# Expert bias of a routed feed-forward layer: split on GpSimd, both parts stacked in one 36-row operand

## The chip, the cores and the metric

One NeuronCore of one Trainium2 chip. The metric is device time in microseconds (us) of one execution. Times inside a trace are us from the start of the span, unless they are given in ns.

## The reference

For x of 2 x 128 tokens of width 512 and a context of 2 x 2048 tokens: x += cross-attention(layernorm(x), context), 16 heads; x += layernorm(self-attention(layernorm(x)) + its input); and a feed-forward layer in which each token goes to one of four experts. What the change touches is in that last part:

```
expert_idx = argmax(x @ W_router)                      # 4 experts
h = gelu(einsum('th,ehi->tei', x, W1) + b1)            # W1 [4, 512, 2048], b1 [4, 2048]
intermediate = einsum('te,tei->ti', onehot, h)
y = layernorm(intermediate @ Wo + bo + x)              # Wo [2048, 512]
```

## The kernel before

The kernel is one block in which each engine has a hand-written list of instructions, in order, tied by semaphores. All DMAs are issued by SyncE (SP), in the order of its own list.

Cross-attention runs to about 354 us. The self-attention that follows has its queries, keys and values in `qkvn` (VectorE adds the bias rows to the PSUM products at L609). They go to HBM and back in another layout (`qkvp`, L257 and L259). Then VectorE runs four additions with all operands in SBUF (`u` at L614, `x_sb` at L615, for each of two batches), one small memset, and the copies of the transposed keys from PSUM into the block-diagonal tile `KM` (L626), on which the score matmuls (L949) wait. `KM` was zeroed by GpSimd (L313) as soon as cross-attention's last weighted values were done. GpSimd otherwise does only the `rsqrt` of each layernorm (L293) there.

The feed-forward layer computes fp32 products from fp32r parts. An operand is split in two: the high part is a rounding copy, the low part is the difference. For tile n of sixteen (four experts, four k tiles each), `split_w1(n)` on VectorE writes `w1H` (L662) and `w1L` (L664) from `w1raw`, which has two buffers; PE then runs 24 matmuls of 512 columns (L1014 to L1016) into all eight PSUM banks: two batches, four column chunks, three part products. `zH` and `zL` are the tokens masked for one expert (`masked_tokens(e)`, L709), for expert 0 ahead of the tiles and for expert e + 1 after `split_w1(4e + 1)`. `split_w1(0)` is far ahead, at 438 us. VectorE may overwrite the buffers of tile n once PE has counted `w1_tile` for tile n - 2.

The bias enters as matmuls that open the accumulation of each bank: `ohT`, the transposed one-hot of the tokens (4 rows), against `b1H` and against `b1L` (4 x 2048 each), L1003. VectorE makes `b1H` (L699) and `b1L` (L701) between `yTL` (L696) and the evacuation of `ohT` (L703).

SP's list, in the order that matters: the last `rows` of biases after cross-attention (L253), the round trips of `qkvn` (L257, L259), `b1raw` (L260), the round trips of the attention's output, then W1 tile n as soon as `w1_split` counts n - 1, and after tile 3 the whole second matrix `woF` (4 MB, 32 KB in each partition, L273):

```python
sp.wait_ge(w1_split, n - 1)
sp.dma_start(w1raw[n % 2][:], w1_v[n]).then_inc(w1_in[n % 2], 16)
if n == 3:
    sp.wait_ge(o2_mm, B)
    sp.wait_ge(b1_split, 2)
    sp.dma_start(woF[:], a["ffn_Wo"]).then_inc(woF_in, 16)
```

The byte ranges matter too: `woF` takes 0 to 32 KB of each partition, `b1raw` 8 to 16 KB before the change.

Of the kernel before, what the change touches and what calls it, by code (L numbers as in the profile page):

```python
# [11 lines left out]
F32 = mybir.dt.float32  # L12
F32R = mybir.dt.float32r
ALU = mybir.AluOpType
# [9 lines left out]
def perceiver_block(nc, a, out):  # L24
# [23 lines left out]
    with ExitStack() as ctx:  # L48
# [3 lines left out]
        def at(name, shape, dtype, kb):  # L52
            return nc.alloc_sbuf_tensor_at(name, shape, dtype, offset=base + int(kb * KB))

        def sem(name):
            return ctx.enter_context(nc.semaphore(name))
# [57 lines left out]
        QT2 = at("QT2", [P, G2, P], F32, 185)  # L114
        zH = at("zH", [P, NW1, TOK], F32R, 136)
        zL = at("zL", [P, NW1, TOK], F32R, 152)
        b1raw = at("b1raw", [E, I], F32, 8)
        b1H = at("b1H", [E, I], F32R, 168)
        b1L = at("b1L", [E, I], F32R, 176)
        mask = at("mask", [P, E, TOK], F32, 185)  # L120
        ohT = at("ohT", [E, B, P], F32R, 189.5)
        wr = at("wr", [P, KT, E], F32, 191)
        hid = at("hid", [P, B, I], F32, 168)

# [5 lines left out]
        def cols(n):  # L130

            col[0] += n
            assert col[0] <= 384
            return small[:, col[0] - n:col[0]]
# [16 lines left out]
        order = cols(E)  # L151
        rank = cols(B * E).rearrange("p (b e) -> p b e", b=B)
        rmax = cols(B)
        onehot = cols(B * E).rearrange("p (b e) -> p b e", b=B)

        ps = ctx.enter_context(nc.psum_tensor("ps", [P, 8, CH], F32))
        T_BANKS = (4, 5)
# [2 lines left out]
        QK2_BANKS = (2, 0)  # L160
        CT_BANKS = (2, 0)
        NP = B * G
        HALF = KT // 2
        WARM = 14
        NOT_YET = 3.0e38
# [29 lines left out]
        cT_mm, cT_done, o2_mm, x2T_mm, x2T_done = (sem(n) for n in ("cT_mm", "cT_done", "o2_mm", "x2T_mm", "x2T_done"))  # L195
        logit_mm, z_ready, ohT_mm, ohT_ready, zT_mm = (sem(n) for n in ("logit_mm", "z_ready", "ohT_mm", "ohT_ready", "zT_mm"))
        z_hi, z_split, w1_hi, w1_split, b1_hi = (sem(n) for n in ("z_hi", "z_split", "w1_hi", "w1_split", "b1_hi"))
        b1_split, w1_tile, w1_mm, gelu_done, hT_mm = (sem(n) for n in ("b1_split", "w1_tile", "w1_mm", "gelu_done", "hT_mm"))
        hT_act, hT_dve, f_mm, out_ready, stored = (sem(n) for n in ("hT_act", "hT_dve", "f_mm", "out_ready", "stored"))
        yT_hi, yT_lo, mask_mm, mask_done, resid_done = (  # L200
            sem(n) for n in ("yT_hi", "yT_lo", "mask_mm", "mask_done", "resid_done"))
# [14 lines left out]
        @block.sync  # L216
        def _(sp):
            sp.dma_start(wk_raw[:, :, 0:P], a["xWk"][:, :, 0:P]).then_inc(wk_in, 16)
            for h in range(2):
                k = slice(HALF * h, HALF * (h + 1))  # L220
                sp.dma_start(raw[0][:, k, :], a["ctxT"][0][:, k, :]).then_inc(raw0_in[h], 16)
            sp.dma_start(bias3, a["bias3"]).then_inc(bias_in, 16)
            for h in range(2):
                k = slice(HALF * h, HALF * (h + 1))
                sp.dma_start(wv_raw[:, k, :], a["xWv"][:, k, :]).then_inc(wv_half_in[h], 16)
            sp.dma_start(x[:], a["x"].rearrange("b t d -> t b d")).then_inc(x_in, 16)
            sp.dma_start(raw[1][:], a["ctxT"][1]).then_inc(raw_in[1], 16)
            sp.dma_start(wq[:], a["xWq"]).then_inc(wq_in, 16)
            for c in range(2, C):
                sp.dma_start(raw[c][:], a["ctxT"][c]).then_inc(raw_in[c], 16)  # L230
            sp.dma_start(wk_raw[:, :, P:D], a["xWk"][:, :, P:D]).then_inc(wk_rest_in, 16)
            for c in range(C):

                sp.wait_ge(k_mm, C * (G - 1) + c + 1)
                sp.dma_start(raw[c][:], a["ctxT"][C + c]).then_inc(raw_in[c], 16)

            sp.wait_ge(v_mm, B * C * JT)
            sp.dma_start(wo[:], a["xWo"]).then_inc(wo_in, 16)
            sp.dma_start(wq2[:], a["wq"]).then_inc(wqkv2_in, 16)
            sp.wait_ge(k_mm, NP * C)  # L240
            sp.dma_start(wk2[:], a["wk"]).then_inc(wqkv2_in, 16)
            sp.dma_start(wv2[:], a["wv"]).then_inc(wqkv2_in, 16)
            sp.dma_start(wo2[:], a["wo"]).then_inc(wo2_in, 16)
            w1_v = a["W1"].rearrange("e (k p) i -> (e k) p i", p=P)
            for n in range(2):
                sp.dma_start(w1raw[n][:], w1_v[n]).then_inc(w1_in[n], 16)
            sp.wait_ge(s_mm, NP * C * HPG)
            for n in range(2):
                sp.dma_start(rowsA[:, n, :], a["rows"][n:n + 1, :].to_broadcast([P, D])).then_inc(rowsA_in, 16)
            sp.dma_start(wr[:], a["W_router"]).then_inc(wr_in, 16)  # L250
            sp.wait_ge(pv_mm, NP * C)
            for n in range(8):
                sp.dma_start(rows[:, n, :], a["rows"][2 + n:3 + n, :].to_broadcast([P, D])).then_inc(rows_in, 16)  # L253

            for b in range(B):
                sp.wait_ge(qkv_ready, 3 * (b + 1))
                sp.dma_start(qkv_by_token[b], qkvn[:, b, :, :]).then_inc(qkv_out[b], 16)  # L257
                sp.wait_ge(qkv_out[b], 16)
                sp.dma_start(qkvp[:, b, :, :, :], qkv_by_position[b]).then_inc(qkv_in[b], 16)  # L259
            sp.dma_start(b1raw[:], a["b1"]).then_inc(b1_in, 16)  # L260
            for b in range(B):
                sp.wait_ge(c2_ready, b + 1)
                sp.dma_start(c_by_position[b], c2[b][:]).then_inc(c2_out[b], 16)
                sp.wait_ge(c2_out[b], 16)
                sp.dma_start(cn[:, b, :], c_dram[b]).then_inc(c2_in[b], 16)
            for n in range(2, NW1):
                sp.wait_ge(w1_split, n - 1)
                sp.dma_start(w1raw[n % 2][:], w1_v[n]).then_inc(w1_in[n % 2], 16)
                if n == 3:

                    sp.wait_ge(o2_mm, B)
                    sp.wait_ge(b1_split, 2)
                    sp.dma_start(woF[:], a["ffn_Wo"]).then_inc(woF_in, 16)  # L273
            for b in range(B):
                sp.wait_ge(out_ready, b + 1)
                sp.dma_start(out[b], u[:, b, :]).then_inc(stored, 16)
            sp.wait_ge(stored, 16 * B)
# [3 lines left out]
        def _(pool):  # L281
            pool.memset(ident[:], 0.0).then_inc(ident_done, 1)
            pool.memset(minus_half, -0.5).then_inc(half_done, 1)
            for e in range(E):
                pool.memset(order[:, e:e + 1], float(E - e)).then_inc(half_done, 1)
            pool.wait_ge(ident_done, 1)
# [1 line left out]
                               pattern=[[-1, P]], channel_multiplier=1).then_inc(ident_done, 1)  # L288

            def rsqrt(n):  # L290
                pool.wait_ge(half_done, 1 + E)
                pool.wait_ge(var_done, n + 1)
                pool.tensor_tensor(rstd[:, n:n + 1], vareps[:, n:n + 1], minus_half, ALU.pow).then_inc(rstd_done, 1)  # L293

# [17 lines left out]
            pool.wait_ge(pv_mm, NP * C)  # L312
            pool.memset(KM[:], 0.0).then_inc(km_zero, 1)  # L313
            pool.wait_ge(km_zero, 1)
            for n in range(B, NLN):
                rsqrt(n)


# [130 lines left out]
        def _(dve):  # L449
# [206 lines left out]

            def split_w1(n):

                dve.wait_ge(w1_in[n % 2], 16 * (n // 2 + 1))
                if n >= 2:  # L660
                    dve.wait_ge(w1_tile, n - 1)
                dve.tensor_copy(w1H[n % 2][:], w1raw[n % 2][:]).then_inc(w1_hi, 1)  # L662
                dve.wait_ge(w1_hi, n + 1)
                dve.tensor_tensor(w1L[n % 2][:], w1raw[n % 2][:], w1H[n % 2][:].bitcast(F32),  # L664
                                  ALU.subtract).then_inc(w1_split, 1)
# [12 lines left out]
                statistics(x2[:, b, :], EPS, 2 * B + 2 * b + 1)  # L678
                normalize(x2[:, b, :], y[:, b, :], 2 * B + 2 * b + 1)

            dve.wait_ge(half_done, 1 + E)
            for b in range(B):
                dve.wait_ge(logit_mm, b + 1)
                step(dve.tensor_copy(logit[:, b, :], ps[:, 6 + b, 0:E]))
# [3 lines left out]
            step(dve.tensor_tensor(rank, rank, order.rearrange("p (o e) -> p o e", o=1).to_broadcast([P, B, E]),  # L688
                                   ALU.mult))
            step(dve.tensor_reduce(rmax, rank, AX.X, ALU.max))  # L690
            dve.tensor_tensor(onehot, rank, wide(rmax), ALU.is_equal).then_inc(z_ready, 1)

            for b in range(B):
                t = slice(b * T, (b + 1) * T)
                dve.wait_ge(yT_hi, b + 1)
                dve.tensor_tensor(yTL[:, :, t], ps[:, 2 + b, :].rearrange("p (k t) -> p k t", k=KT),  # L696
                                  yTH[:, :, t].bitcast(F32), ALU.subtract).then_inc(yT_lo, 1)
            dve.wait_ge(b1_in, 16)
            dve.tensor_copy(b1H[:], b1raw[:]).then_inc(b1_split, 1)  # L699
            dve.wait_ge(b1_split, 1)  # L700
            dve.tensor_tensor(b1L[:], b1raw[:], b1H[:].bitcast(F32), ALU.subtract).then_inc(b1_split, 1)  # L701
            dve.wait_ge(ohT_mm, 1)
            dve.tensor_copy(ohT[:], ps[0:E, 1, 0:TOK].rearrange("p (b t) -> p b t", b=B)).then_inc(ohT_ready, 1)  # L703

            def masked_tokens(e):

# [35 lines left out]
        def _(pe):  # L742
# [238 lines left out]
                product(ps[:, 6 + b, 0:E], [(yT[:, k, b * T:(b + 1) * T], wr[:, k, :]) for k in range(KT)])\  # L981
                    .then_inc(logit_mm, 1)

            pe.wait_ge(z_ready, 1)
            for e in range(E):
                for b in range(B):
                    last = pe.matmul(ps[:, 4 + e // 2, (e % 2) * TOK + b * T:(e % 2) * TOK + (b + 1) * T],
# [1 line left out]
                if e % 2:  # L989
                    last.then_inc(mask_mm, 1)  # L990
            for b in range(B):
                last = pe.transpose(ps[0:E, 1, b * T:(b + 1) * T], onehot[:, b, :], ident[:])
            last.then_inc(ohT_mm, 1)


            pe.wait_ge(ohT_ready, 1)
            pe.wait_ge(b1_split, 2)
            pe.wait_ge(mask_done, E // 2)
            pe.wait_ge(yT_lo, B)
            for b in range(B):  # L1000
                for c in range(IC):
                    for n, part in enumerate((b1H, b1L)):
                        pe.matmul(ps[:, IC * b + c, :], ohT[:, b, :], part[:, c * CH:(c + 1) * CH],  # L1003
                                  start=(n == 0), stop=False)
            for n in range(NW1):
                pe.wait_ge(z_split, 2 * (n // KT + 1))
                pe.wait_ge(w1_split, n + 1)
# [73 lines left out]
```

## Time and profile before

| | |
|---|---|
| median of 3 runs | 606.34 us (604.85 to 606.74) |
| the profiled execution's own time | 605.77 us |
| its span, first to last instruction | 604.0 us |
| mean granted clock of TensorE | 0.936 |
| PE (matmul) busy | 539.8 us, 89% |
| VectorE busy | 303.3 us, 50% |
| ScalarE busy | 159.0 us, 26% |
| GpSimd busy | 40.6 us, 7% |

The span leaves out 1.77 us of the profiled execution's time. PE's busy share is an average over stages: between 393 and 470 us the engines take turns on one chain, and PE is idle for much of it; from 476 to 564 us it runs the sixteen W1 tiles without a break. A granted clock of 1.00 is 2.4 GHz and one of 0.50 is 1.2 GHz.

### The profile page before, as it was taken

Reading aid. Unit: us, or ns where it says so; the run is one execution under the profiler, and the core shown is the slowest. Engines: PE = TensorE matmul, PEld = TensorE weight load, DVE = VectorE, ACT = ScalarE, POOL = GpSimd, SP = SyncE. Lnnn points to the kernel's source line nnn. Section 1 sums busy time; section 2 is a strip of 40 time slices with the busy share of each in tenths; the row PEclk is TensorE's granted clock in tenths of the full one; section 3 lists DMA queues with packets and bytes.
Section 4 is the critical chain, followed back from the end, with each engine's and each line's share of the span. In section 5 each row is a group of like instructions: output and inputs, shape, how many; then the busy total and the mean of one; then the engine's idle time right before and its main releaser. Section 6 shows DMA issues by size and latency. Waiting matters only on the chain.

```text
span 604.0 us, 8313 instructions
## 1 busy us (share of the span) xinstructions
PE 539.8 (89%) x3406; PEld 390.3 (65%) x3406; DVE 303.3 (50%) x542; ACT 159.0 (26%) x232; POOL 40.6 (7%) x32
## 2 busy tenths in 40 slices
PE   5999999999989899999998768955875999999995
PEld 4777767777767688777775543432734788888642
DVE  4545336576757311275757133174356679766122
ACT  3110053736363420136373610012101100000400
POOL 0300000003930000000000020000000000000000
PEclk9999999999989999999999678976875799999999
DMA  8500000004300000300006340440130475553000
GB/s 289 234 0 1 1 1 1 2 2 159 122 0 3 1 0 1 139 3 2 1 1 267 119 137 3 104 106 0 27 113 0 175 311 195 209 174 120 1 5 30
DMA packets 25820, 46.18 MB, mean 76 GB/s; under 512 B 17588, under 2 KB 18612, under 8 KB 21940
## 3 DMA queue, kind: packets, MB, share of 16 engines
q1 hardware_dynamic: 25784, 45.66, 21.7%
q8 instruction: 27, 0.44, 0.3%
q14 instruction: 9, 0.07, 0.0%
HBM read 43.04 MB, written 2.62 MB: 76 GB/s over the span
## 4 chain that ended last, share of the span: by engine, by line
PE 82%; DVE 9%; DMA 2%; issue 2%; ACT 2%; POOL 0%; SPq 0%; POOLq 0%; DVEq 0%
PE ps L752 42%; PE ps L809 10%; PE ps L795 6%; PE ps L1014 5%; PE ps L824 5%; PE ps L1016 5%; PE ps L1015 5%; PE ps L949 2%; DMA wv_raw<-in_xWv 2%; PE ps L1003 1%; DVE KM L626 1%; ACT Pm L341 1%; DVE Pm L502 1%; DVE small L460 1%; DVE small L639 1%
## 5 line engine op out<-in xcount | busy, mean ns | idle before, releaser
L349 ACT COPY PT<-ps 128x512 f32<-128x512 f32 x96 | 53.3, 587 | 101.1 <-PE ps L809 101.1
L809 PE MATMUL ps<-ident,Pm 128*128 128x128 f32 x512 | 72.0, 284 | 3.7 <-ACT PT L349 2.2
L809 PEld LDWEIGHTS ps<-ident,Pm 128*128 128x128 f32 x512 | 58.4, 144 | 24.0 <-issue 16.9
L502 DVE TENSOR_SCALAR_CACHE_REDUCE Pm<-ps,small 128x512 f32<-128x512 f32 x96 | 66.4, 747 | 8.7 <-PE ps L795 8.7
L341 ACT ACTIVATE Pm<-Pm,small 128x2048 f32<-128x2048 f32 x32 | 64.1, 2006 | 14.2 <-DVE Pm L502 14.2
L752 PE MATMUL ps<-ctxH,wkH 128*128 128x512 f32 x124 | 52.0, 420 | 2.4 <-DVE Kr L482 1.9
L752 PE MATMUL ps<-wvH,ctxH 128*128 128x512 f32 x128 | 50.0, 391 | 1.1 <-DVE wvL L546 1.1
L1014 PE MATMUL ps<-w1H,zH 128*128 128x512 f32 x128 | 50.6, 395 | 0.0
L1016 PE MATMUL ps<-w1H,zL 128*128 128x512 f32 x128 | 50.3, 393 | 0.0
L1015 PE MATMUL ps<-w1L,zH 128*128 128x512 f32 x128 | 50.3, 393 | 0.0
L752 PE MATMUL ps<-wvH,ctxL 128*128 128x512 f32 x128 | 49.8, 389 | 0.0
L752 PE MATMUL ps<-wvL,ctxH 128*128 128x512 f32 x128 | 49.8, 389 | 0.0
L752 PE MATMUL ps<-ctxL,wkH 128*128 128x512 f32 x124 | 49.1, 396 | 0.0
L752 PE MATMUL ps<-ctxH,wkL 128*128 128x512 f32 x124 | 49.0, 395 | 0.0
L482 DVE TENSOR_SCALAR Kr<-ps,small 128x512 f32<-128x512 f32 x32 | 24.0, 749 | 47.3 <-PE ps L752 47.3
L491 DVE COPY V<-ps 128x512 f32<-128x512 f32 x16 | 11.1, 691 | 62.1 <-PE ps L752 62.1
L511 DVE COPY PT<-ps 128x512 f32<-128x512 f32 x32 | 22.1, 691 | 36.5 <-PE ps L809 35.7
L752 PEld LDWEIGHTS ps<-ctxH,wkH 128*128 128x128 f32 x124 | 23.6, 191 | 21.1 <-issue 17.1
L795 PE MATMUL ps<-Kr,qT 32*128 32x512 f32 x256 | 36.5, 640 | 0.6 <-ACT qT L368 0.6
L664 DVE TENSOR_TENSOR w1L<-w1raw,w1H 128x2048 fp32r<-128x2048 f32 x16 | 36.7, 2294 | 0.6
L824 PE MATMUL ps<-PT,V 128*32 128x128 f32 x1024 | 34.7, 276 | 0.9 <-DVE PT L511 0.9
L824 PEld LDWEIGHTS ps<-PT,V 128*32 128x32 f32 x1024 | 26.1, 110 | 8.6 <-issue 5.9
(150 smaller groups left out, 682.4 us busy)
## 6 DMA issues: line engine op xcount, KB each, us to landing
w1raw<-in_W SPq DMA_DIRECT2D x16, 1024.0 KB, 4.8
raw<-in_ctxT SPq DMA_DIRECT2D x7, 1024.0 KB, 4.7
woF<-in_ffn_Wo SPq DMA_DIRECT2D x1, 4096.0 KB, 14.0
rows<-in_rows SPq DMA_DIRECT2D x8, 256.0 KB, 5.3
qkv_dram<-qkvn SPq DMA_DIRECT2D x2, 768.0 KB, 3.5
qkvp<-qkv_dram SPq DMA_DIRECT2D x2, 768.0 KB, 5.5
raw<-in_ctxT SPq DMA_DIRECT2D x2, 512.0 KB, 6.3
wv_raw<-in_xWv SPq DMA_DIRECT2D x2, 512.0 KB, 8.8
```

Of the source, the lines that this page charges most:

```text
L341: act.activation(Pm[:, i, :], Pm[:, i, :], ACT.Exp, bias=mx[:, p % 2, i, C - 1:C], scale=-1.0, accum_out=den[:, p, i:i + 1]).then_inc(exp_ ...
L349: act.copy(PT[:, c % 2, i, :, :].rearrange("p k t -> p (k t)"), ps[:, T_BANKS[i % 2], :]).then_inc(pt_act, 1)
L482: dve.tensor_scalar(Kr[:, c, :], ps[:, K_BANK, :], bias3[:, 1, p % G:p % G + 1], None, ALU.add).then_inc(k_done, 1)
L502: dve.tensor_scalar(Pm[:, i, c * CH:(c + 1) * CH], ps[:, i, :], -1.0, mx[:, p % 2, i, c - 1:c] if c else NOT_YET, ALU.mult, ALU.min, accum ...
L664: dve.tensor_tensor(w1L[n % 2][:], w1raw[n % 2][:], w1H[n % 2][:].bitcast(F32), ALU.subtract).then_inc(w1_split, 1)
L752: mm = pe.matmul(dst, l, r, start=(n == 0), stop=(n == len(pairs) - 1))
L795: pe.matmul(ps[:, i, :], qT[q, g, b * T:(b + 1) * T], Kr[q, c, :], start=True, stop=True)\
L809: last = pe.transpose(ps[:, T_BANKS[i % 2], j * P:(j + 1) * P], Pm[:, i, c * CH + j * P:c * CH + (j + 1) * P], ident[:])
L824: last = pe.matmul(ps[q, PV_BANK, 0:T], V[:, c * JT + j, (HPG * g + i) * DH:(HPG * g + i + 1) * DH], PT[:, c % 2, i, j, :], start=(c == 0 ...
L1014: pe.matmul(dst, zH[:, n, t], wH[:, cc], start=False, stop=False)
L1015: pe.matmul(dst, zH[:, n, t], wL[:, cc], start=False, stop=False)
L1016: last = pe.matmul(dst, zL[:, n, t], wH[:, cc], start=False, stop=(n == NW1 - 1))
```

## The change

The one-hot is written twice on VectorE, into columns 0 to 3 and 32 to 35 of a 36-column tile, which GpSimd zeroes at the start of the kernel. Its transpose, `ohT`, has 36 rows. `b1raw` has 36 rows too, is zeroed by GpSimd after `KM` and filled by two DMAs (rows 0 to 3 and 32 to 35), which SP now issues ahead of the `rows` transfers and behind a wait for that memset. GpSimd makes `b1HL`: a rounding copy of all 36 rows, then rows 32 to 35 become the difference; it starts once all six products of queries, keys and values are done. One matmul for each bank takes the place of two. `b1raw` moves to 96 KB, in the buffer that `split_w1(0)` later writes, so that split waits for the bias; `b1HL` lies at 8 KB, under `woF`, so `woF`'s transfer waits for PE's first W1 tile.

```diff
@@ SP
             sp.wait_ge(pv_mm, NP * C)
+            sp.wait_ge(b1_zero, 1)
+            for n in range(2):
+                sp.dma_start(b1raw[DH * n:DH * n + E, :], a["b1"]).then_inc(b1_in, 16)
             for n in range(8):
                 sp.dma_start(rows[:, n, :], ...).then_inc(rows_in, 16)
...
-            sp.dma_start(b1raw[:], a["b1"]).then_inc(b1_in, 16)
...
                 if n == 3:
-                    sp.wait_ge(o2_mm, B)
-                    sp.wait_ge(b1_split, 2)
+                    sp.wait_ge(w1_tile, 1)
                     sp.dma_start(woF[:], a["ffn_Wo"]).then_inc(woF_in, 16)
@@ GpSimd
+            pool.memset(onehot, 0.0).then_inc(half_done, 1)
...
             pool.wait_ge(km_zero, 1)
-            for n in range(B, NLN):
+            pool.memset(b1raw[:], 0.0).then_inc(b1_zero, 1)
+            for n in range(B, 2 * B):
+                rsqrt(n)
+            pool.wait_ge(b1_in, 32)
+            pool.wait_ge(qkv_mm, QKV_PRODUCTS)
+            pool.tensor_copy(b1HL[:], b1raw[:]).then_inc(b1_hi2, 1)
+            pool.wait_ge(b1_hi2, 1)
+            low = slice(DH, E2)
+            pool.tensor_tensor(b1HL[low, :], b1raw[low, :], b1HL[low, :].bitcast(F32), ALU.subtract).then_inc(b1_split, 1)
+            for n in range(2 * B, NLN):
                 rsqrt(n)
@@ VectorE
             def split_w1(n):
+                if n == 0:
+                    dve.wait_ge(b1_split, 1)
...
-            dve.tensor_tensor(onehot, rank, wide(rmax), ALU.is_equal).then_inc(z_ready, 1)
+            for n in range(2):
+                dve.tensor_tensor(onehot[:, :, DH * n:DH * n + E], rank, wide(rmax), ALU.is_equal).then_inc(z_ready, 1)
...
-            dve.wait_ge(b1_in, 16)
-            dve.tensor_copy(b1H[:], b1raw[:]).then_inc(b1_split, 1)
-            dve.wait_ge(b1_split, 1)
-            dve.tensor_tensor(b1L[:], b1raw[:], b1H[:].bitcast(F32), ALU.subtract).then_inc(b1_split, 1)
             dve.wait_ge(ohT_mm, 1)
-            dve.tensor_copy(ohT[:], ps[0:E, 1, 0:TOK]...).then_inc(ohT_ready, 1)
+            dve.tensor_copy(ohT[:], ps[0:E2, 1, 0:TOK]...).then_inc(ohT_ready, 1)
@@ PE
-            pe.wait_ge(z_ready, 1)
+            pe.wait_ge(z_ready, 2)
...
-                last = pe.transpose(ps[0:E, 1, b * T:(b + 1) * T], onehot[:, b, :], ident[:])
+                last = pe.transpose(ps[0:E2, 1, b * T:(b + 1) * T], onehot[:, b, :], ident[:])
...
-                    for n, part in enumerate((b1H, b1L)):
-                        pe.matmul(ps[:, IC * b + c, :], ohT[:, b, :], part[:, c * CH:(c + 1) * CH],
-                                  start=(n == 0), stop=False)
+                    pe.matmul(ps[:, IC * b + c, :], ohT[:, b, :], b1HL[:, c * CH:(c + 1) * CH], start=True, stop=False)
```

## Rows read from the trace of the kernel before

**Rows 1.** The page, part 4: the chain that ended last, shares by engine.

```profile
...
PE 82%; DVE 9%; DMA 2%; issue 2%; ACT 2%; POOL 0%; SPq 0%; POOLq 0%; DVEq 0%
...
```

**Rows 2.** The chain of waits, 392 to 400: start, us, what.

```profile
...
393.79 0.61 DVE u L614
...
396.74 0.61 DVE KM L626
...
```

**Rows 3.** Timeline, 392 to 403: start, us, engine, line, operation, idle before.

```profile
...
393.09 0.69 DVE L609 TENSOR_TENSOR qkvn<-ps,rows 128x512 f32<-128x512 f32 x1 [2.74 <-PE ps L752]
...
397.76 3.62 SPq L260 DMA_DIRECT2D b1raw<-in_b  x1
...
```

**Rows 4.** Timeline, 145 to 148, GpSimd and VectorE.

```profile
...
145.53 1.89 POOL L308 CAST ctxH<-raw 128x2048 fp32r<-128x2048 f32 x1 [114.53 <-DMA raw<-in_ctxT]
145.55 0.28 DVE L530 TENSOR_TENSOR attnT<-ps,RT 128x128 f32<-128x128 f32 x1
...
145.86 1.64 DVE L532 TENSOR_SCALAR attnT<-attnT,small 128x128 f32<-128x128 f32 x1
...
147.50 4.56 POOL L310 TENSOR_TENSOR ctxL<-raw,ctxH 128x2048 fp32r<-128x2048 f32 x1
...
```

**Rows 5.** Source view of line 521: count, duration ns min/median/max, first and last start.

```profile
...
L521 DVE COPY rexp<-small x8: 226/227/2768, 112.4 to 352.4; 128x128 f32<-128x128 f32 x8
...
```

**Rows 6.** Timeline, 353 to 358.

```profile
...
353.55 3.65 SPq L253 DMA_DIRECT2D rows<-in_rows  x8
353.58 3.51 POOL L313 MEMSET KM<- 128x4096 f32 x1 [182.05 <-PE ps L824]
...
354.58 2.59 DVE L532 TENSOR_SCALAR attnT<-attnT,small 128x128 f32<-128x128 f32 x1
354.78 3.14 DVE L599 TENSOR_TENSOR x_sb<-x_sb,rowsA 128x512 f32<-128x512 f32 x2
...
```

**Rows 7.** Timeline of VectorE, 359 to 377.

```profile
...
376.00 0.69 DVE L609 TENSOR_TENSOR qkvn<-ps,rowsA 128x512 f32<-128x512 f32 x1 [5.63 <-PE ps L752]
```

**Rows 8.** The chain of waits, 464 to 477.

```profile
...
466.58 1.13 DVE b1H L699
...
470.40 5.65 PE ps L1003 x16
...
```

**Rows 9.** Timeline, 468 to 477.

```profile
...
468.93 0.38 PE L992 MATMUL ps<-ident,small 128*4 128x128 f32 x2
469.13 0.58 ACT L435 COPY mask<-ps 128x512 f32<-128x512 f32 x1 [1.00 <-PE ps L987]
...
469.94 0.40 DVE L703 CAST ohT<-ps 4x256 fp32r<-4x256 f32 x1
...
471.41 1.21 DVE L709 TENSOR_TENSOR zL<-yTL,mask 128x1024 fp32r<-128x1024 f32 x1
...
475.98 0.80 PE L1014 MATMUL ps<-w1H,zH 128*128 128x512 f32 x1
...
476.55 0.36 SPq L273 DMA_DIRECT2D woF<-in_ffn_Wo  x1
...
```

**Rows 10.** Windows: length, busy of PE, PEld, DVE, ACT, POOL; granted clock; DMA share, GB/s.

```profile
...
472.24:479.07 6.83, 6.83 (x17) 4.85 (x16) 6.07 (x5) 0.00 (x0) 0.00 (x0) 0.50 0.27 83
...
```

**Rows 11.** DMA view, issued 476 to 478, then 486 to 488: us to landing.

```profile
...
woF<-in_ffn_Wo SPq DMA_DIRECT2D x1, 4096.0 KB, 14.0
w1raw<-in_W SPq DMA_DIRECT2D x1, 1024.0 KB, 4.8
...
w1raw<-in_W SPq DMA_DIRECT2D x1, 1024.0 KB, 7.0
```

**Rows 12.** Timeline of VectorE, 483 to 511.

```profile
...
483.27 1.23 DVE L662 CAST w1H<-w1raw 128x2048 fp32r<-128x2048 f32 x1 [4.92 <-PE ps L1016]
...
494.15 1.23 DVE L662 CAST w1H<-w1raw 128x2048 fp32r<-128x2048 f32 x1 [1.88 <-PE ps L1016]
...
507.52 2.29 DVE L664 TENSOR_TENSOR w1L<-w1raw,w1H 128x2048 fp32r<-128x2048 f32 x1
...
```

More of the change, by code:

```diff
@@ L116, in perceiver_block @@
         zL = at("zL", [P, NW1, TOK], F32R, 152)
-        b1raw = at("b1raw", [E, I], F32, 8)
-        b1H = at("b1H", [E, I], F32R, 168)
-        b1L = at("b1L", [E, I], F32R, 176)
+        E2 = DH + E
+        b1raw = at("b1raw", [E2, I], F32, 96)
+        b1HL = at("b1HL", [E2, I], F32R, 8)
         mask = at("mask", [P, E, TOK], F32, 185)
-        ohT = at("ohT", [E, B, P], F32R, 189.5)
+        ohT = at("ohT", [E2, B, P], F32R, 189.5)
         wr = at("wr", [P, KT, E], F32, 191)
@@ L153, in perceiver_block @@
         rmax = cols(B)
-        onehot = cols(B * E).rearrange("p (b e) -> p b e", b=B)
+        onehot = cols(B * E2).rearrange("p (b e) -> p b e", b=B)
         ps = ctx.enter_context(nc.psum_tensor("ps", [P, 8, CH], F32))
@@ L162, in perceiver_block @@
         NP = B * G
+        QKV_PRODUCTS = 3 * B
         HALF = KT // 2
@@ L197, in perceiver_block @@
         z_hi, z_split, w1_hi, w1_split, b1_hi = (sem(n) for n in ("z_hi", "z_split", "w1_hi", "w1_split", "b1_hi"))
-        b1_split, w1_tile, w1_mm, gelu_done, hT_mm = (sem(n) for n in ("b1_split", "w1_tile", "w1_mm", "gelu_done", "hT_mm"))
+        b1_zero, b1_hi2, b1_split, w1_tile, w1_mm, gelu_done, hT_mm = (sem(n) for n in ("b1_zero", "b1_hi2", "b1_split", "w1_tile", "w1_mm", "gelu_done", "hT_mm"))
         hT_act, hT_dve, f_mm, out_ready, stored = (sem(n) for n in ("hT_act", "hT_dve", "f_mm", "out_ready", "stored"))
@@ L290, in rsqrt @@
             def rsqrt(n):
-                pool.wait_ge(half_done, 1 + E)
+                pool.wait_ge(half_done, 2 + E)
                 pool.wait_ge(var_done, n + 1)
@@ L679, in _ @@
                 normalize(x2[:, b, :], y[:, b, :], 2 * B + 2 * b + 1)
-            dve.wait_ge(half_done, 1 + E)
+            dve.wait_ge(half_done, 2 + E)
             for b in range(B):
@@ L697, in _ @@
                                   yTH[:, :, t].bitcast(F32), ALU.subtract).then_inc(yT_lo, 1)
-            dve.wait_ge(b1_in, 16)
-            dve.tensor_copy(b1H[:], b1raw[:]).then_inc(b1_split, 1)
-            dve.wait_ge(b1_split, 1)
-            dve.tensor_tensor(b1L[:], b1raw[:], b1H[:].bitcast(F32), ALU.subtract).then_inc(b1_split, 1)
             dve.wait_ge(ohT_mm, 1)
-            dve.tensor_copy(ohT[:], ps[0:E, 1, 0:TOK].rearrange("p (b t) -> p b t", b=B)).then_inc(ohT_ready, 1)
+            dve.tensor_copy(ohT[:], ps[0:E2, 1, 0:TOK].rearrange("p (b t) -> p b t", b=B)).then_inc(ohT_ready, 1)
             def masked_tokens(e):
@@ L991, in _ @@
             for b in range(B):
-                last = pe.transpose(ps[0:E, 1, b * T:(b + 1) * T], onehot[:, b, :], ident[:])
+                last = pe.transpose(ps[0:E2, 1, b * T:(b + 1) * T], onehot[:, b, :], ident[:])
             last.then_inc(ohT_mm, 1)
             pe.wait_ge(ohT_ready, 1)
-            pe.wait_ge(b1_split, 2)
+            pe.wait_ge(b1_split, 1)
             pe.wait_ge(mask_done, E // 2)
```

## The prediction

> **What bounds the kernel now.** I read the chain of waits first. Its shares say that PE carries most of the end and VectorE 9% [rows 1], but these are averages, and the edits fall in three places. At 393 to 400 us the chain in order of time shows VectorE alone: the four additions in SBUF begin at 393.79 and the copies into `KM` at 396.74, with nothing but 0.02 us gaps between [rows 2]. GpSimd is idle there. At 466 to 476 us the chain runs through VectorE's bias split, from 466.58, and through the sixteen bias matmuls, 5.65 us [rows 8]. From 476 to 564 us PE is the chain; the timeline of VectorE shows what could displace it, the supply of split W1 tiles [rows 12].
>
> **The split leaves VectorE; one product goes.** Without the split VectorE waits for the transposed one-hot. PE ends the two transposes at 468.93 + 0.38 = 469.31; `ohT` started at 469.94 [rows 9]. The second one-hot write costs about 0.1 us ahead of PE, so `ohT` starts near 469.5. The mask copy ends at 469.71 [rows 9], 469.8 with that 0.1, so masking starts 0.4 earlier and `zL`, which ended at 472.62, ends near 472.2. Eight bias matmuls at the 0.23 us spacing of the first ones (at 2.4 GHz they would be done by 471.9) no longer last. A matmul's spacing goes by its 512 columns, so I give 36 rows the price of 4. The first W1 matmul moves from 475.98 to 472.25: 3.7 us.
>
> The granted clock decides what tile 0 makes of that. It is 0.50 from 472.24 to 479.07, after PE had idled between the one-hot's transposes and the bias [rows 9, 10], where a matmul takes 0.43 us; at full clock a tile of 24 takes (494.15 - 483.27) / 2 = 5.44 us, 0.227 each [rows 12]. With one such stretch of 3.4 us before the W1 matmuls have brought the clock back, tile 0 is done at 475.65 + 16 x 0.227 = 479.3, against 483.2 before: 3.9 us won. If the clock stays low until 479.07 it is 480.9, if it never falls 477.7.
>
> **`woF` moves behind tile 0.** It was issued at 476.55 [rows 9] and landed 14.0 us later, at 490.55; W1 tile 4, issued at 486.86, took 7.0 us and landed at 493.9, 3.3 us after `woF` [rows 11]: transfers on SP's queue follow each other. VectorE's split of tile 4 began at 494.15 [rows 12], so it had 0.3 us to spare. Now `woF` is issued at 479.35. W1 tile 3 ahead of it is issued at 475.7, when split 1 is done. Before, its 4.8 us [rows 11] ended at 480.9, so `woF` takes 9.65 us behind a predecessor; alone it needs some 1.5 us more (4.8 - 3.3). It lands at 490.5 and tile 4 at 493.8; from a later first byte, up to 495. But PE, 3.9 us ahead, would want tile 4's split begun at 490.3. From that split on VectorE works without a pause: split 4, four additions, split 5, masking, split 6, from 494.15 to 507.52 + 2.29 = 509.81, when PE's tile 6 begins 0.6 us later at 510.4 [rows 12]. The same 15.7 us behind 493.8 to 495 give 509.5 to 510.7. So the 3.9 us come back as PE waiting ahead of tiles 4 to 6, and what is left at tile 6 is -0.9 to +0.3 us; I take -0.4. With the two other clocks it is -1.3 (tile 3's transfer becomes the floor) to +1.6.
>
> **GpSimd's work at 393 us.** It waits for the sixth product, so it starts as VectorE starts the last `qkvn` addition, 393.09 [rows 3]. GpSimd's copy of 2048 columns took 1.89 us and its subtraction 4.56 us on 128 partitions [rows 4]. No row has either on 36 or 4 partitions. VectorE's own copy of 4 x 2048 took 1.13 us to the next start [rows 8], as long as 128 partitions do (1.23, rows 12), so I take GpSimd's prices unchanged: 393.15 to 395.05, then 4.56. The lower bound is near nothing for the subtraction.
>
> What meets it is VectorE's chain. While GpSimd's copy ran at 145.53, an addition with a PSUM operand took its plain 0.28 us, and the next instruction, all in SBUF, was held until 147.50: 1.64 us [rows 4]. A copy in SBUF that takes 0.227 us took 2.77 once [rows 5]. Under the memset of `KM`, two more SBUF instructions were held (2.59, and one of the two in 3.14) until it ended [rows 6]. Every SBUF-only instruction that met a long GpSimd one was held, every one with PSUM was not. The four additions are SBUF-only; `qkvn` and `KM` have PSUM operands. But the held ones at [rows 4] and [rows 5] have one tensor source, and of those with two only L599 met GpSimd, behind a held one. So bounds: nothing if two sources are free of this, and for the rest as follows. The first addition waits from 393.70 until 395.05 and ends at 395.65. GpSimd's subtraction, ready meanwhile, takes its turn: 395.65 to 400.2. The second addition ends at 400.85, the third and fourth at 402.3, `KM` starts at 402.4, not 396.74: **+5.7 us**. Nothing behind it has slack: the score matmuls wait for `KM`, and everything down to 470 us is a chain.
>
> The Trainium skill, "SBUF — State Buffer", section "SBUF: two separate sides", has a rule that speaks against this change: VectorE and GpSimd share a pair of ports under an exclusive lock for a whole instruction, and a VectorE instruction with two SBUF inputs falls under it against a GpSimd instruction that reads SBUF. By it the sum holds the 5.7 us; by the other reading of [rows 4, 5], that only single-source copies are held, it holds none.
>
> **What costs nothing.** The memset of 36 x 2048 takes half of `KM`'s 3.51 us [rows 6], 357.1 to 358.9. The copy at L532 on which PE's output product waits got in between two GpSimd instructions at 147.50 [rows 4], and I expect so at 357.1; otherwise PE's output product starts 1.8 us later. SP's eight `rows` issues move from 353.55 behind that memset and two bias issues. One bias issue took 3.62 us in SP's queue, behind the `qkvp` transfer [rows 3]; with 0.4 to 3.6 each, `rows` starts at 359.8 to 366.2, takes 3.65 us to issue and some 5.3 to land, by 375.2 at the latest, and the first use is at 376.00 [rows 7]. Without that cover each late microsecond would count in full. GpSimd's waits hold up only its own next `rsqrt`, at 448 us. `split_w1(0)` at 438 us finds the bias split at 400.2. The memset of the one-hot is 0.1 us at the start.
>
> **Sum.** +5.7 at `KM`, -0.4 at tile 6: +5.3. The profiled execution's own time is 605.77 (span 604.0 and 1.77 outside it), 0.57 below the runs' median of 606.34. The sum gives 611.1 on the one and 611.6 on the other; I take 611.3, so 606.0 as the time without a change. About 0.3%, 1.8 us, is what measurement of this kernel can tell from no change.
>
> **The rivals.**
> - VectorE keeps its turn: its second addition follows the first within 0.04 us, so all four run before GpSimd's subtraction. For it: the gaps of [rows 2] are that short. Against it: GpSimd asks first. Then `KM` moves by 1.3 us only: +1.3 - 0.4 = +0.9, 606.9.
> - No hold on two-source instructions: -0.4, 605.6. For it: no row shows one held by itself. Against it: L599 in [rows 6]. It decides as soon as the additions keep 0.69 us.
> - The win of the 3.9 us is kept, because tile 4 lands before 490.3 or so: then -3.9 alone, 602.1, faster, with no hold; with it +5.7 - 3.9 = +1.8, 607.8. It decides at tile 4's landing: each us before 494.15 is won, down to 490.3. Against it: `woF` alone needs 9.65 us, and it is issued 2.8 us later than before.
> - The clock: a low stretch twice as long behind the bias makes each case up to 2 us worse.
>
> **Chances.** Forecast 0.54; VectorE keeps its turn 0.18; no hold 0.14; win kept without a hold 0.07, with it 0.07. The forecast's own range is 609.8 to 613.3: the clock's -0.9 to +2.0 around 611.3, and less if the subtraction on 4 rows is short. The range reaches down over the second and third case to 604.5 and leaves out the kept win below it and about a tenth above. Faster: 0.12, the kept win and the clock's luck in the third case. Same: 0.33, the second and third case and part of the last. Slower: 0.55.
>
> **What would show it.** In the profile after: L614 or L615 with a row of several us beside GpSimd's two new instructions near 393 to 400; the first `KM` copy near 402.4; L1003 eight times; the first W1 matmul 3.7 us nearer to the one-hot; PE idle on VectorE's `w1L` ahead of tile 4, and VectorE's split 4 released by a transfer rather than by PE. I am wrong if the additions show 0.69 us, if GpSimd's subtraction on 4 rows is far below 4.56 us, or if tile 4 is there in time.

## The result and the profile after

The changed kernel takes 611.6 us (median of 4 runs, 610.54 to 613.8), the kernel before 605.94 us: ratio 1.0098, 95% interval 1.0069 to 1.0127. In run e10 below, beside runs of its own of the kernel before, the same kernel gave 1.010 (1.0072 to 1.0127). The forecast was 611.3 us. The profiled execution took 611.71 us with a span of 609.9 us, 5.9 us more than before.

GpSimd's timeline of the changed kernel, from the bias split on (start, us):

```profile
392.59 1.88 POOL L323 CAST b1HL<-b1raw 36x2048 fp32r<-36x2048 f32 x1 [23.49 <-PE ps L763]
394.56 4.82 POOL L326 TENSOR_TENSOR b1HL<-b1raw,b1HL 4x2048 fp32r<-4x2048 f32 x1
```

The chain of waits of the changed kernel over the same time answers to [rows 2]:

```profile
392.49 0.69 DVE qkvn L621
393.19 1.85 DVE u L626
395.04 0.03 issue
395.06 4.87 DVE x_sb L627
399.94 0.02 issue
399.96 0.70 DVE u L626
400.66 0.03 issue
400.69 0.69 DVE x_sb L627
...
401.56 0.61 DVE KM L638
```

The first addition stands beside GpSimd's copy and ends 0.57 us behind it; the second stands beside the subtraction and ends at 399.92, 0.54 us behind its 399.38. Both wait for GpSimd; below, this wait is called the hold. The third and fourth are plain, at 0.69 us. The first `KM` copy starts 9.00 us behind the last `qkvn` addition, where it was 3.58 us (396.67 - 393.09): 5.42 us of hold.

The second place, the W1 tiles: VectorE's timeline of the changed kernel, to hold against [rows 12].

```profile
485.40 1.23 DVE L676 CAST w1H<-w1raw 128x2048 fp32r<-128x2048 f32 x1 [3.67 <-PE ps L1025]
...
490.84 1.23 DVE L676 CAST w1H<-w1raw 128x2048 fp32r<-128x2048 f32 x1 [1.89 <-PE ps L1025]
...
500.17 1.23 DVE L676 CAST w1H<-w1raw 128x2048 fp32r<-128x2048 f32 x1 [5.78 <-DMA w1raw<-in_W]
...
516.07 1.23 DVE L676 CAST w1H<-w1raw 128x2048 fp32r<-128x2048 f32 x1 [0.24 <-PE ps L1025]
```

The four rows are splits 2, 3, 4 and 7. VectorE was idle for 5.78 us before split 4, and a transfer released it, no longer PE. PE then waits 2.26 us for that split, the first such wait in the tiles. SP's timeline has `woF` at 485.32, when tile 0 is done, and W1 tile 4 at 488.98. The DMA view of the changed kernel, for these two (us from issue to landing):

```profile
woF<-in_ffn_Wo SPq DMA_DIRECT2D x1, 4096.0 KB, 12.4
...
w1raw<-in_W SPq DMA_DIRECT2D x1, 1024.0 KB, 11.2
```

Tile 4 took 7.0 us before [rows 11]; it now lands at 500.2, 2.5 us behind `woF`.

The third place, the windows of the changed kernel around the one-hot (length, busy of PE, PEld, DVE, ACT, POOL, granted clock, DMA share, GB/s), to hold against [rows 10]:

```profile
462.00:473.00 11.00, 6.93 (x30) 6.18 (x30) 3.48 (x14) 1.77 (x4) 0.55 (x1) 0.50 0.00 0
473.00:481.97 8.97, 8.46 (x21) 5.98 (x20) 8.38 (x7) 1.75 (x2) 0.00 (x0) 0.50 0.19 47
481.97:485.40 3.43, 3.43 (x17) 2.84 (x16) 0.00 (x1) 0.00 (x0) 0.00 (x0) 1.00 0.45 191
```

The same for the kernel before, ahead of the stretch in [rows 10]:

```profile
468.83:472.24 3.41, 2.32 (x12) 1.66 (x12) 3.41 (x4) 1.87 (x2) 0.00 (x0) 1.00 0.02 7
```

After the change the granted clock is at 0.50 through the one-hot's matmuls, the bias and most of tile 0. Before, it was at full for the mask's last matmuls and the first bias matmuls. In the chain after, the eight bias matmuls take 3.78 us, 0.43 us apart; in e3 below, at full clock, they take 2.08 us.

How far each stage ran, in the traces of this and of the experiments. Columns: from the last `qkvn` addition to the first `KM` copy; from there to the self-attention's first output (`c2`, L654 before); from there to the first comparison of the one-hot (L687 before); and from that comparison to the end of tile 0 (start of split 2), to the start of split 4, and to the first copy of `hidT` (the transposed hidden layer) behind all tiles. All in us, from starts in VectorE's timeline.

| kernel | qkvn to KM | KM to c2 | c2 to one-hot | to tile 0's end | to split 4 | to hidT |
|---|---|---|---|---|---|---|
| before | 3.58 | 35.85 | 32.09 | 18.66 | 29.54 | 101.07 |
| changed | 9.00 | 35.02 | 31.65 | 17.24 | 32.01 | 103.41 |
| e10, changed again | 9.00 | 35.01 | 31.66 | 17.24 | 31.87 | 103.26 |
| e1, GpSimd later | 3.58 | 35.87 | 32.00 | 15.07 | 29.53 | 100.93 |
| e2, before, woF late | 3.58 | 35.85 | 32.04 | 18.67 | 33.50 | 105.30 |
| e3, e1 and woF in eight | 3.58 | 35.83 | 32.06 | 15.07 | 25.95 | 97.48 |
| e4, before, GpSimd copies | 6.33 | 38.88 | 32.83 | 18.65 | 29.53 | 101.06 |
| e5, before, GpSimd memsets | 3.58 | 35.88 | 31.98 | 18.64 | 29.52 | 101.05 |
| e6, woF early | 3.58 | 35.86 | 32.10 | 15.08 | 28.09 | 99.49 |
| e7, e3 with 16 matmuls | 3.58 | 35.92 | 32.06 | 18.22 | 29.10 | 100.63 |
| e8, before, woF in eight | 3.58 | 36.35 | 31.99 | 20.24 | 31.12 | 102.65 |
| e9, changed, woF in eight | 8.99 | 35.02 | 31.64 | 17.24 | 28.12 | 99.64 |

For the changed kernel: +5.42, -0.83, -0.44 and +2.34 (103.41 - 101.07) are +6.49; 0.60 us had been gained by the last `qkvn` addition (392.49, not 393.09), a part that the change's timing doesn't explain. The sum is 5.89, what the first copy of `hidT` moved by (565.68 to 571.57).

### The profile page after: what moved, and what is told of

Read it like the earlier page. It is cut to its first block, busy times and chain, and to the rows that moved or that the text cites. A ratio compares the mean times of both kernels' runs of the same rounds, so it can differ in the third digit from the quotient of the medians.

```text
span 609.9 us, 8303 instructions
## 1 busy us (share of the span) xinstructions
PE 539.8 (89%) x3398; PEld 391.2 (64%) x3398; DVE 305.9 (50%) x541; ACT 159.0 (26%) x232; POOL 49.2 (8%) x36
## 4 chain that ended last, share of the span: by engine, by line
PE 80%; DVE 11%; DMA 3%; issue 3%; ACT 2%; POOL 0%; SPq 0%; POOLq 0%; DVEq 0%; ACTq 0%
PE ps L763 41%; PE ps L820 10%; PE ps L806 6%; PE ps L835 5%; PE ps L1023 4%; PE ps L1025 4%; PE ps L1024 4%; DMA w1raw<-in_W 2%; PE ps L944 2%; PE ps L960 2%; DMA wv_raw<-in_xWv 2%; DVE w1L L678 1%; DVE x_sb L627 1%; DVE KM L638 1%; DVE Pm L514 1%
## 5 line engine op out<-in xcount | busy, mean ns | idle before, releaser
L676 DVE CAST w1H<-w1raw 128x2048 fp32r<-128x2048 f32 x16 | 19.6, 1224 | 24.8 <-PE ps L1025 16.6
```

## The experiments

Each ratio is to the kernel before, run on the same chip, with its 95% interval.

**e1: GpSimd's split later.** The changed kernel with one more wait.

```diff
             pool.wait_ge(qkv_mm, QKV_PRODUCTS)
+            pool.wait_ge(v2_ready, 3)
```

> The changed kernel with one more wait: GpSimd's bias split starts after both copies of V2, about 413, when all of VectorE's instructions have a PSUM operand. Theory (the hold of two-source SBUF additions costs the time): the four additions keep 0.69 us each, the first KM copy is 3 us behind the last qkvn addition again, and the time falls by 4.8 to 5.7 us, from 611.6 to about 606.3. Rival (the additions are long for another reason, such as the bias or qkvp transfers on the DMA queues at that time): they stay long and the time stays near 611. In both, tile 4 of W1 still waits for its transfer behind woF.

604.7 us, ratio 0.9994 (0.9972 to 1.0015). VectorE's and GpSimd's rows in its timeline:

```profile
393.10 0.68 DVE L627 TENSOR_TENSOR u<-y,rows 128x512 f32<-128x512 f32 x1
393.81 0.69 DVE L628 TENSOR_TENSOR x_sb<-x_sb,rows 128x512 f32<-128x512 f32 x1
...
408.25 0.69 DVE L653 TENSOR_TENSOR P<-ps,small 128x512 f32<-128x512 f32 x1
...
409.62 4.51 POOL L327 TENSOR_TENSOR b1HL<-b1raw,b1HL 4x2048 fp32r<-4x2048 f32 x1
```

All additions are plain, and the softmax's subtractions (L653), which read PSUM, keep 0.69 us beside GpSimd. The whole loss is gone: 1.0098 against 0.9994 is 6.3 us, more than the 4.8 to 5.7 us that were expected. The table has the parts: against the changed kernel 5.42 us less of hold, 1.20 us more in the two stages behind it, and 2.48 us less from the one-hot to `hidT`, where the clock is at full again for the one-hot's last matmuls. The same GpSimd work costs nothing 15 us later.

**e4 and e5: the hold alone, on the kernel before.** Two GpSimd instructions of 128 x 2048 are added at the sixth product, in regions that are dead by then; `woF`'s transfer, 80 us later, waits for them too.

```diff
+            for n in range(B, 2 * B):
+                rsqrt(n)
+            pool.wait_ge(qkv_mm, 3 * B)
+            for n in range(2):
+                pool.tensor_copy(wk2[:], wq2[:]).then_inc(extra, 1)     # e4
+                pool.memset(wk2[:], 0.0).then_inc(extra, 1)             # e5
+                pool.wait_ge(extra, n + 1)
-            for n in range(B, NLN):
+            for n in range(2 * B, NLN):
                 rsqrt(n)
```

> The kernel before plus two GpSimd copies of 128 x 2048 fp32 from SBUF to SBUF (1.9 us each), started when the sixth product is done; nobody but woF's transfer waits for them, 80 us later. Theory (the hold alone costs the time): the first addition is held to the end of the first copy, the second to the end of the second, KM moves by 2.5 to 3.3 us and the time by the same, about 608.8. Rival: no hold on additions with two SBUF operands, 605.9.

> As the run with the two GpSimd copies, but with two memsets of 128 x 2048 (1.8 us each), which write SBUF and read nothing. If any long GpSimd instruction holds an addition with two SBUF operands, KM moves by 2.3 to 3.1 us, about 608.6. If only those that read SBUF hold it (the Trainium skill, 'SBUF - State Buffer', says so), the additions keep 0.69 us and the time stays at 605.9.

e4: 611.73 us, 1.011 (1.0078 to 1.0143). e5: 604.84 us, 1.0007 (0.9983 to 1.0032). Their timelines, e4 first:

```profile
391.08 4.19 POOL L321 COPY wk<-wq 128x2048 f32<-128x2048 f32 x2 [21.96 <-PE ps L760]
391.66 1.86 DVE L622 TENSOR_TENSOR u<-y,rows 128x512 f32<-128x512 f32 x1
...
393.55 2.26 DVE L623 TENSOR_TENSOR x_sb<-x_sb,rows 128x512 f32<-128x512 f32 x1
395.85 0.69 DVE L622 TENSOR_TENSOR u<-y,rows 128x512 f32<-128x512 f32 x1
```

```profile
391.32 3.67 POOL L321 MEMSET wk<- 128x2048 f32 x2 [23.33 <-PE ps L760]
391.90 0.68 DVE L622 TENSOR_TENSOR u<-y,rows 128x512 f32<-128x512 f32 x1
...
392.62 0.69 DVE L623 TENSOR_TENSOR x_sb<-x_sb,rows 128x512 f32<-128x512 f32 x1
```

Beside copies the first two additions take 1.86 and 2.26 us, beside memsets 0.68 and 0.69. So an addition with two SBUF operands is held by the GpSimd instructions that read SBUF (copy, subtraction), and not by the one that only writes it (memset). The Trainium skill, "SBUF — State Buffer", section "SBUF: two separate sides", names just this exception, and these rows agree with it. Single-source VectorE instructions are another matter: beside the memset of `KM`, L532 took 2.59 us [rows 6]. L599, the addition with two SBUF sources in those rows, stood behind L532 and not behind the memset itself.

The hold of e4 is 2.75 us (6.33 - 3.58), as expected, but the time rose by 6.7 us. The table says where: 3.0 us more from `KM` to `c2`, for the same work, and 0.7 us more from there to the one-hot (38.88 and 32.83, where the kernel before has 35.85 and 32.09). The windows over that stage, e4 and then e5:

```profile
397.38:436.26 38.88, 25.46 (x89) 15.97 (x89) 20.07 (x32) 7.52 (x13) 0.00 (x0) 0.63 0.11 18
```

```profile
394.88:430.76 35.88, 22.46 (x89) 13.41 (x90) 19.92 (x33) 7.51 (x13) 0.11 (x1) 0.71 0.15 24
```

PE's 89 matmul records are the same, the mean granted clock is 0.63 instead of 0.71, and PE is busy 3.0 us longer. All four runs of e4 had a mean clock of 0.923 to 0.926 over the whole kernel, and those of the kernel before beside them 0.929 to 0.944. In the changed kernel that stage was 0.8 us shorter than before:

```profile
401.49:436.51 35.02, 21.00 (x89) 13.54 (x89) 19.99 (x33) 7.52 (x13) 0.00 (x0) 0.79 0.01 2
```

So a shift on this chain of short PE bursts went together with a change of the clock, in either direction. How the one brings about the other was not tried.

**e2: only woF's wait, on the kernel before.**

```diff
                     sp.wait_ge(o2_mm, B)
                     sp.wait_ge(b1_split, 2)
+                    sp.wait_ge(w1_tile, 1)
                     sp.dma_start(woF[:], a["ffn_Wo"]).then_inc(woF_in, 16)
```

> The kernel before, with woF's transfer behind PE's first W1 tile, and nothing else. Theory (what falls behind woF in SP's queue takes the win): woF issued near 483.3 instead of 476.6, tile 4's transfer lands 4 us late (498), VectorE's 15.7 us from split 4 to split 6 follow, PE's tile 6 begins 3.3 us late: +3 to +4 us, about 609.4. Rival (the transfers share the DMA engines and tile 4 slips in beside woF): tile 4 lands in time and the time stays at 605.9.

608.96 us, 1.0067 (1.0044 to 1.0091). `woF` is issued at 482.39 and tile 4 at 485.98; split 4, from its timeline:

```profile
497.22 1.23 DVE L663 CAST w1H<-w1raw 128x2048 fp32r<-128x2048 f32 x1 [5.83 <-DMA w1raw<-in_W]
```

Tile 4 lands 11.2 us after its issue, split 4 is 4.0 us late (33.50 against 29.54), and the end of the tiles 4.2 us. The transfers follow each other.

**e3: woF in eight transfers.** With e1's wait.

```diff
-                if n == 3:
-                    sp.wait_ge(w1_tile, 1)
-                    sp.dma_start(woF[:], a["ffn_Wo"]).then_inc(woF_in, 16)
+                if 4 <= n < 12:
+                    k = slice(2 * (n - 4), 2 * (n - 3))
+                    sp.dma_start(woF[:, k, :], a["ffn_Wo"][:, k, :]).then_inc(woF_in, 16)
...
-            pe.wait_ge(woF_in, 16)
+            pe.wait_ge(woF_in, 8 * 16)
```

> GpSimd's split after the second copy of V2, and woF in eight transfers of 512 KB, one behind each of the W1 tiles 4 to 11, instead of one of 4 MB behind tile 3. Theory (what the earlier start of tile 0 wins is lost to the wait for tile 4): no split waits for a transfer, the 3.6 to 3.9 us of tile 0 last to the end, about 3.7 us under the kernel before: ratio 0.994. Rival (PE's start of tile 0 is given back elsewhere, in the clock or in VectorE's chain): ratio 0.998 or more.

600.2 us, 0.9927 (0.9901 to 0.9952): the fastest version, 0.73% under the kernel before. VectorE's split 4 in it:

```profile
490.43 1.23 DVE L676 CAST w1H<-w1raw 128x2048 fp32r<-128x2048 f32 x1 [1.89 <-PE ps L1025]
```

PE releases it again, and the 3.6 us that tile 0 ends earlier (15.07 against 18.66) are 3.6 us at `hidT` (97.48 against 101.07).

**e6: woF early again, in one transfer.** `b1HL` moves out of `woF`'s range, and GpSimd's split waits for the last score matmul.

```diff
-        b1HL = at("b1HL", [E2, I], F32R, 8)
+        b1HL = at("b1HL", [E2, I], F32R, 144)
...
-            pool.wait_ge(qkv_mm, QKV_PRODUCTS)
+            pool.wait_ge(s2_mm, G2)
...
-                    sp.wait_ge(w1_tile, 1)
+                    sp.wait_ge(o2_mm, B)
```

> b1HL at 144 KB, where nothing of woF lies, filled by GpSimd after the last score matmul; woF waits for the attention's output alone and is issued right behind tile 3, in one transfer. Theory (transfers on this queue follow each other): woF cannot begin before tile 3 is in, tile 4 lands about 17.5 us after tile 3's issue and split 4 still waits 3 us for it, so only 1 to 1.3 us are won against the kernel before: ratio 0.998. Rival (only the wait for the first W1 tile holds woF up, and without it the whole 3.7 us are won): ratio 0.994.

603.4 us, 0.9964 (0.9942 to 0.9987). `woF` is issued at 476.52, and split 4 still waits:

```profile
493.15 1.23 DVE L676 CAST w1H<-w1raw 128x2048 fp32r<-128x2048 f32 x1 [4.01 <-DMA w1raw<-in_W]
```

At `hidT` 1.6 us are won, where 1.0 to 1.3 were expected and e3 wins 3.6. The interval leaves the rival's 0.994 out only by 0.0002; the trace's wait of 4.01 us decides.

**e7: sixteen matmuls on top of e3.** Each of the eight is run twice, so this kernel adds the bias twice.

```diff
-                    pe.matmul(ps[:, IC * b + c, :], ohT[:, b, :], b1HL[:, c * CH:(c + 1) * CH], start=True, stop=False)
+                    for n in range(2):
+                        pe.matmul(ps[:, IC * b + c, :], ohT[:, b, :], b1HL[:, c * CH:(c + 1) * CH],
+                                  start=(n == 0), stop=False)
```

> As the run with woF in eight transfers, but each of the eight 36-row bias matmuls is run twice (the bias is added twice, so the output differs by that). It asks how much of the win is the eight matmuls and how much is the split that left VectorE. Theory: eight matmuls of 0.23 to 0.43 us are 1.8 to 3.4 us, of which 0.3 hide behind zL: 1.5 to 3.2 us slower than with eight, ratio 0.997 to 0.999 to the kernel before. Rival (the matmuls were hidden by masking anyway, and the win is all from the split): as fast as with eight, 0.994.

604.85 us, 1.0001 (0.9986 to 1.0016), the kernel before's time: nearly the whole win of e3 is the eight matmuls, and next to nothing is the split that left VectorE. It is also more than expected (3.15 us at tile 0's end, 0.74% in the ratios). PE's timelines, e7 and then e3, show the pieces:

```profile
470.13 5.25 PE L1014 MATMUL ps<-b1HL,ohT 36*128 36x512 f32 x16 [0.66 <-DVE ohT L714]
475.30 0.79 PE L1025 MATMUL ps<-w1H,zH 128*128 128x512 f32 x1
```

```profile
469.94 2.08 PE L1013 MATMUL ps<-b1HL,ohT 36*128 36x512 f32 x8 [0.66 <-DVE ohT L714]
472.13 0.72 PE L1023 MATMUL ps<-w1H,zH 128*128 128x512 f32 x1
```

The spacing at full clock is 0.23 us with 36 rows, as with 4 rows before. And the windows behind it, e7 and then e3:

```profile
472.36:479.17 6.81, 6.81 (x17) 4.89 (x16) 5.60 (x4) 0.00 (x0) 0.00 (x0) 0.50 0.37 113
```

```profile
472.24:475.63 3.39, 3.39 (x8) 2.62 (x9) 3.35 (x3) 0.00 (x0) 0.00 (x0) 0.50 0.00 0
475.66:479.07 3.41, 3.41 (x17) 2.81 (x16) 2.15 (x2) 0.00 (x0) 0.00 (x0) 1.00 0.60 228
```

With eight matmuls the low stretch is 3.4 us long, with sixteen 6.8 us, as before the change. In both PE is busy all the time. So the 3.15 us are not all matmuls. An estimate from these rows: eight more at 0.23 us are 1.8 us, of which 0.3 hide behind `zL` by the expectation, and 3.4 us more at half the clock cost 1.7 us, 3.2 us in all.

**e8: woF in eight transfers on the kernel before.** e3's edit, behind the waits that `woF` had.

> The kernel before with woF in the same eight transfers and nothing else. Theory: tile 4 was in time before (0.3 us to spare), so nothing is won: ratio 1.000 within 0.001. Rival (the one transfer of 4 MB cost something before too, and the win of the run with eight transfers is not the bias's): as fast as that run, 0.994.

606.57 us, 1.0021 (1.0004 to 1.0038). Nothing is won, so e3's win is not that of smaller transfers by themselves. It is somewhat slower than expected. In its trace the tiles behind tile 0 run as in the kernel before, and tile 0 ends 1.6 us later, in a low stretch of the clock of 10.2 us where the kernel before has 6.83 [rows 10]:

```profile
472.70:482.90 10.20, 10.20 (x25) 7.48 (x24) 6.37 (x5) 0.00 (x0) 0.00 (x0) 0.50 0.32 103
```

The edit acts only behind tile 3, so it does not explain why the clock stayed low. This trace is of the slowest of e8's twelve runs. It warns that one trace of a kernel doesn't settle how long such a stretch is.

**e9 and e10: the two causes in the changed kernel.** e9 is the changed kernel with e3's eight transfers, e10 the changed kernel itself on the same chip.

> The changed kernel with woF in eight transfers behind tiles 4 to 11, GpSimd's split where the change put it. Theory (two causes that add up, the hold at 393 and the wait for tile 4): no wait for tile 4, hold as before, so the changed kernel's time less 3.5 to 6 us: ratio to the kernel before 1.001 to 1.005. Rival (the hold's delay makes woF's transfer harmless, since everything is later): as the changed kernel, 1.010.

> The changed kernel itself, unchanged, beside the one with eight transfers on the same chip: ratio to the kernel before 1.007 to 1.013. Theory: the granted clock stays at 0.50 through the one-hot's matmuls and the bias and tile 0 ends some 17 us after the one-hot, as in its first profile, since the hold moves this stage. Rival (that clock was the luck of one execution): tile 0 ends 15 us after the one-hot.

e9: 607.93 us, 1.0048 (1.0026 to 1.0071). e10: 611.11 us, 1.010 (1.0072 to 1.0127). The transfers are worth 0.5% here. The hold (9.00) and tile 0's end (17.24) are in e10 what they were in the first profile, to 0.01 us, so the low clock at the one-hot was not the luck of one execution. e9 makes three traces with the hold in the changed kernel, all at 17.24; the three without it and with eight bias matmuls (e1, e3, e6) are at 15.07 or 15.08. Against e3, e9 is 1.2% slower, with 5.4 us of hold and 2.2 us more at the one-hot and tile 0.

## Why the prediction was right

- **The hold of the additions.** Forecast +5.7 us at `KM`, measured +5.42. The copy on 36 rows took 1.88 us (forecast 1.89), the subtraction on 4 rows 4.51 us where nothing met it (forecast 4.56). e1 takes the hold away and with it the loss; e4 makes it in the kernel before.
- **Who gets the turn.** GpSimd, as the forecast had it. The second addition was issued 0.03 us behind the first and was held for the whole subtraction; in e4 too, for the second copy. The rival in which VectorE keeps its turn falls.
- **Which instructions are held.** "Every SBUF-only instruction that met a long GpSimd one was held" went too far. e5's additions met memsets and kept 0.68 and 0.69 us. The change's two GpSimd instructions both read SBUF, so the forecast did not suffer from it.
- **What hid the other edits.** The second memset took 1.80 us (356.30 to 358.10) and L544 kept its 2.59 us beside the first. The two bias issues took 0.63 us together, so `rows` began at 358.86, ahead of the forecast's 359.8 to 366.2. The first `qkvn` addition still waited for PE.
- **The first W1 matmul.** Forecast 3.7 us earlier from the one-hot. In e1 and e3 it is 7.6 us behind the one-hot's first comparison instead of 11.4, which is 3.7 us. In the changed kernel it is 9.33: 2.0 us.
- **The tail is the term that was mis-sized.** "-0.4 at tile 6" measured +2.34 at `hidT` (tile 6 itself starts 47.81 us behind the one-hot instead of 45.76: +2.05), outside its own bounds of -1.3 to +1.6. Its mechanism held where the hold is absent: e1 shows -0.14, and tile 0's end at 15.07 where the forecast's 479.3 means 14.7. The 3.4 us of low clock in it were half of the stretch in [rows 10], and no row that the prediction names gave that length; e3 shows 3.39. Of the tail's two parts the wait for tile 4 was sized well: split 4 loses 3.89 us to it (+2.47 against tile 0's -1.42) and in e2 3.96, where 490.3 against 493.8 to 495 means 3.5 to 4.7. The part that failed is the gain at tile 0: 3.9 us forecast, 1.42 us measured (18.66 to 17.24). The cause is the clock behind the hold. I took the low stretch of the kernel before, longer or shorter, and did not ask what a 5.7 us shift does to the clock during the mask's matmuls and the bias. It was low for all of them, tile 0 ended 2.2 us later than in e1, and with it `woF`, tile 4 and the rest moved. That the hold brings this low clock is shown by e1 and e9 together; by which way it does so stays open, for e4's shift of 2.75 us left this stage at 18.65 us.
- **What evened it out, by luck.** -0.83 us from `KM` to `c2`, with the clock at 0.79 against 0.71. -0.44 us from there to the one-hot, although the mean clock of that stage was lower (0.66 against 0.69): the product behind the round trip alone took 5.11 us at 0.72 instead of 5.76 us at 0.64. And 0.60 us ahead of `qkvn`, within the scatter of that moment: the three traces with the changed kernel's code up to there (this one, e10 and e9) have it at 392.49, 392.04 and 392.97. Without them the total would have been some 613.5 us. The forecast had none of the three, and its 611.3 was closer than its terms.
- **Two causes, not one.** Taking away the hold gives 1.0098 to 0.9994; taking away the wait for tile 4 gives 1.010 to 1.0048; both give 0.9927. What the eight matmuls win is real, and each of the two edits that came with them spent it.

## What to carry to other kernels

Work moved to an idle engine is not free: look which instructions of the other engine stand beside it. Here VectorE's additions in SBUF waited for a GpSimd copy or subtraction to end (1.86 to 4.87 us instead of 0.69), those with a PSUM operand didn't, and a start 15 us later cost nothing. When a large transfer on a queue gets a new wait, look at the small one that is queued behind it and at how much time that one had to spare: here 0.3 us. Then cut the large one into pieces that fit into the gaps. That pays only where the small one is waited for: in e8, where it had been in time, it won nothing.

## What the runs showed of the hardware that was not expected

- GpSimd's time does not fall with the partitions: the fp32 subtraction of 2048 columns took 4.51 us on 4 partitions and 4.56 us on 128 [rows 4], the copy 1.88 on 36 and 1.89 on 128.
- The granted clock in the bias stage: with PE back to back on 4-row or 36-row bias matmuls the clock fell to 0.50, or stayed there. It rose only behind W1 matmuls of 128 rows, and how far behind differs: the first of them and the rise are at 475.98 and 479.07 in the kernel before, 475.30 and 479.17 in e7, 472.13 and 475.64 in e3, 477.49 and 481.97 in the changed kernel, 477.00 and 482.9 in e8. Why the bias matmuls did not bring it back was not tried.
- A shift of 2.75 us cost 6.7 us in e4. One of 5.42 us gave back 1.3 us on its way to the one-hot in the changed kernel, alike in its two profiles (35.02 and 31.65 us, 35.01 and 31.66), and then cost 2.2 us at the one-hot and tile 0.
